# A hardware loop over graphs with two turns in its body in place of one

## The reference: what is computed

```
x = _layernorm(x + _L0_gnn_ref(x, L0_gnn_a, adj, adj), axis=-1)
x = _layernorm(x + _L1_gnn_ref(x, adj, L1_gnn_Wp, ..., L1_gnn_b2), axis=-1)
x = _layernorm(x + _L2_gnn_ref(x, adj, L2_gnn_W, L2_gnn_e, L2_gnn_bias), axis=-1)
x = _layernorm(x + _L3_gnn_ref(x, adj, L3_gnn_W, L3_gnn_a_src, L3_gnn_a_dst), axis=-1)
```

## Time and profile before

| what | value |
|---|---|
| median of 3 runs | 1199.27 us (1198.74 to 1199.39) |
| the profiled execution: its own time | 1201.41 us |
| the profiled execution: span on the core | 1199.5 us |
| share of the span busy: PE, DVE, ACT, POOL | 93%, 90%, 84%, 34% |
| granted TensorE clock over the span | 0.97 of full speed, 1.00 in the loop |

### The profile page before, as it was taken

How to read it: one execution, slowest core, us unless ns; L and a number is a source line. 1 busy time by engine, 2 the same in 40 slices (tenths; PEclk the granted TensorE clock), 3 DMA queues, 4 the chain that set the end, 5 groups by cost and what they waited for, 6 DMA issues and landing times.

```text
span 1199.5 us, 29294 instructions
## 1 busy us (share of the span) xinstructions
PE 1115.1 (93%) x7721; PEld 913.9 (76%) x7752; DVE 1082.1 (90%) x4214; ACT 1012.0 (84%) x2581; POOL 405.5 (34%) x800
## 2 busy tenths in 40 slices
PE   4778999999999999999999999999999999999864
PEld 3456788888777778888777788887777788878653
DVE  6898999999999999999999999999999999997542
ACT  3456799999999999999999999999999999998654
POOL 3122334423334344323433344233343443233211
PEclk9699999999999999999999999999999999999876
DMA  3000011011011111010011110110111100100000
GB/s 84 27 19 28 27 37 36 20 33 35 17 35 35 35 35 33 20 35 26 26 35 35 35 35 17 35 35 18 35 35 35 35 27 25 36 27 11 19 9 18
DMA packets 59459, 35.95 MB, mean 30 GB/s; under 512 B 3872, under 2 KB 54816, under 8 KB 59424
## 3 DMA queue, kind: packets, MB, share of 16 engines
q1 hardware_dynamic: 59424, 35.54, 9.7%
HBM read 18.75 MB, written 8.39 MB: 23 GB/s over the span
## 4 chain that ended last, share of the span: by engine, by line
DVE 46%; issue 28%; POOL 12%; PE 8%; ACT 2%; DVEq 2%; POOLq 0%; DMA 0%; ACTq 0%; SPq 0%
DVE wB L1116 5%; DVE pTB L1147 5%; DVE vA L1226 4%; DVE wE L1116 3%; DVE vA L1245 3%; DVE wE L1134 3%; POOL rirA L450 3%; POOL lnr_E L438 2%; POOL lnr_B L438 2%; DVE lnst_B L1268 2%; DVE lnst_D L1088 2%; DVE lnst_C L1088 2%; DVE t2B L1301 2%; DVE lnst_Z L1088 1%; DVE y_D L1318 1%
## 5 line engine op out<-in xcount | busy, mean ns | idle before, releaser
L750 PE MATMUL ps<-hE,pTE 128*128 128x128 f32 x1024 | 133.7, 279 | 0.1
L432 POOL TENSOR_TENSOR lnve_Z<-lnmv_Z,consts 128x4 f32<-128x4 f32 x32 | 17.1, 534 | 330.8 <-DVE lnmv_Z L1096 330.8
L678 PE MATMUL ps<-xsA,pA 128*128 128x128 f32 x1024 | 124.3, 281 | 1.2 <-ACT xsA L1555 1.2
L750 PE MATMUL ps<-hB,pTB 128*128 128x128 f32 x1024 | 124.9, 275 | 0.0
L750 PEld LDWEIGHTS ps<-hE,pTE 128*128 128x128 f32 x1024 | 122.8, 193 | 2.3 <-issue 0.6
L810 PE MATMUL ps<-att_j,xD 128*128 128x512 f32 x256 | 124.3, 609 | 0.0
L767 PE MATMUL ps<-gin_j,hgat 128*128 128x512 f32 x256 | 121.7, 599 | 0.0
L678 PEld LDWEIGHTS ps<-xsA,pA 128*128 128x128 f32 x1024 | 119.1, 195 | 1.5 <-ACT xsA L1555 1.3
L750 PEld LDWEIGHTS ps<-hB,pTB 128*128 128x128 f32 x1024 | 119.4, 192 | 0.2 <-issue 0.2
L1116 DVE SCALAR_TENSOR_TENSOR wE<-ps,hE,y2E 128x512 f32<-128x512 f32 x128 | 90.0, 745 | 24.8 <-ACT y2E L1577 21.5
L1545 ACT ACTIVATE pA<-vA,nmA,rirA 128x512 f32<-128x512 f32 x128 | 104.6, 818 | 4.7 <-DVE vA L1245 4.7
(11 more groups left out here) (237 smaller groups left out, 3040.9 us busy)
## 6 DMA issues: line engine op xcount, KB each, us to landing
xA<-in_x_dram SPq DMA_DIRECT2D x32, 256.0 KB, 2.6
xrA<-in_x_dram SPq DMA_DIRECT2D x32, 256.0 KB, 2.7
xrB<-xB SPq DMA_DIRECT2D x32, 256.0 KB, 2.2
out_dram<-xout SPq DMA_DIRECT2D x32, 256.0 KB, 2.2
adj_i<-in_adj_dram SPq DMA_DIRECT2D x1, 1024.0 KB, 5.2
a<-in_L_gnn_a_dram SPq DMA_DIRECT2D x2, 64.0 KB, 5.6
w_sb<-in_L_gnn_W_dram SPq DMA_DIRECT2D x2, 64.0 KB, 4.5
l2w<-in_L_gnn_W_dram SPq DMA_DIRECT2D x2, 64.0 KB, 3.7
```

Of the source, the lines that this page charges most:

```text
L678: last = mm(at("aggA")[:, i * P:(i + 1) * P], pA[:, j, i * P:(i + 1) * P], xsA[:, j], start=(j == 0), stop=(j == NT - 1))
L750: last = mm(at("agg" + n)[:, i * P:(i + 1) * P], att[n]["pT"][:, i, j], att[n]["h"][:, j, 0:P], start=(j == 0), stop=(j == NT - 1))
```

## The change

The loop goes over every second turn, and its body holds two turns, the second with the loop's register plus one. It makes 13 passes (turns 6, 8, ..., 30) in place of 26. The order of the steps on every engine and all that they compute stay the same.

```
-            with eng.Fori(LAST_DELAY + 1, GRAPHS) as it:
+            with eng.Fori(LAST_DELAY + 1, GRAPHS - 1, 2) as it:
                 body(Turn(it, GRAPHS))
+                body(Turn(it + 1, GRAPHS))
```

## The result

The changed kernel takes 1240.4 us (median of six runs, 1236.7 to 1244.2). The kernel before took 1199.3 us on the same chip (median of six, 1198.7 to 1199.9). The ratio is 1.034, with a 95% interval of 1.0328 to 1.0353: slower by 41.1 us. The profiled execution of the changed kernel took 1241.05 us, with a span of 1239.2 us.

A forecast was written before the change was run, and what follows sets the result against it. DVE was taken to set the pace: 36.0 us of refetch stalls at 12 jumps less 2.0 us for removed branches gave +34 us, 1199.3 to 1233 us; range 1195.5 to 1254 us, likeliest case alone 1218 to 1250 us.

The forecast's parts named there:

- likeliest case: DVE alone refetches code at its jump back: 1233 us (1218 to 1250), chance 0.52.
- DVE sets the pace, and its place before `lnve_B` is what the change touches.: Steady loop: PE and ACT wait for DVE every turn; DVE's 0.30 us idle at the back edge is affected.
- DVE's pass no longer fits, and the head is fetched again at 12 jumps.: DVE's pass grows from 192 to 371 instructions, 1.5 to 2.9 packets; its first piece is lost at each jump back.
- everything fits: Rival: DVE's store keeps the pass, no refetch; 1197.3 us (chance 0.25) or, with more gain, about 1195.5 us (0.10).
- Idle of 3.3 us, 3.0 more than before, 36.0 us.: Before `lnve_B` at 12 jumps back, 0.30 us idle becomes a 3.3 us fetch, priced from a 64 KB DMA: 36.0 us.
- Nothing else on it is shortened while it stands: the others catch up and wait for it: During DVE's fetch stalls, the other engines only wait, so all 36.0 us of added idle lie on the path.
- The bounds of the fetch: Added idle at DVE's 12 jumps back: 24.0 us at 2.3 us per fetch, 50.4 us at 4.5 us.
- Gain of 2.0 us from the removed edges.: DVE's 13 removed branches save 0.15 us each, limited by a chain over ACT and PE; ends 0 and 4.8 us.
- the sign that was named: Profile after: first turn of a body against second, `y_E` to `cenA`, 8.5 us without a branch, 8.7 with it.
- the second turn's saved register operations: Fewer register operations in a body's second turn, issued beside running work: counted at nothing, at most 0.7 us back.
- The branches of ACT, PE, POOL and SP cost nothing.: Back edges on the engines other than DVE cost nothing now; ACT's lies within 0.87 us of waiting for PE.
- ACT misses too: Rival: ACT also refetches at its back edge, 2.1 us per jump reaching DVE, 26 us more, 1259 us; ACT or PE 0.13.

The follow-up runs named there:

- place 13: Changed kernel with DVE's loop head moved to instruction 13 of its 128-instruction packet, so a pass ends with the third packet: 1192.56 us, 0.9945 of the kernel before.
- the delay on DVE: Changed kernel with DVE's loop head at the start of a packet and two needless multiplications on DVE ending each pass: 1229.53 us, 1.0248 of the kernel before.
- place 8: Changed kernel with DVE's loop head moved to instruction 8 of its 128-instruction packet, so a pass touches three packets: 1191.67 us, 0.9942 of the kernel before.
- the padded kernel: Changed kernel, DVE's head at 8 in its packet, ACT's pass lengthened by 60 fulfilled waits, ACT's head at 111, touching four packets: 1266.63 us.
- place 14: Changed kernel with DVE's loop head at instruction 14 of its packet, so only the branch lies in a fourth packet: 1256.65 us, 1.0472 of the kernel before.
- ACT padded, place 60: Changed kernel, DVE's head at 8 in its packet, ACT's pass lengthened by 60 fulfilled waits, ACT's head at 60, touching three packets: 1212.67 us.

## Why the prediction was right, and where its sizes were off

The forecast was 1233 us; 1240.4 us came, within the range and within the likeliest case's own (1218 to 1250 us). The mechanism was right. That the number is so close owes something to luck: the fetch was put 4.8 us too high and the clock's 14.2 us were missing, and the two errors partly cancel. Point by point:

- **DVE sets the pace, and its place before `lnve_B` is what the change touches.** Right. DVE alone doubled gives 1.0328, all others doubled 0.9993.
- **DVE's pass no longer fits, and the head is fetched again at 12 jumps.** Right, and so was the reason: four touched packets plus the one ahead are five, and the store holds four. The place at which it decides was sharper than the text said: not the 2.9 packets of code, but where in a packet the loop begins. The rival "everything fits" was given the condition that the store holds four or five packets; that contradicts this count, since with four and the head behind place 13 the kernel misses unless it is hinted, and with four and the head at place 13 or before it fits. And the 129 instructions to a packet were counted from the 20 packets within the span, while six more of 8 KB had come in the 11 us before it; the places 13 and 14 give 128.
- **Idle of 3.3 us, 3.0 more than before, 36.0 us.** The idle is 2.90 us, 2.60 more, 31.2 us. The row taken, a load of 64 KB, was 0.4 us too slow a stand-in; the small load's 2.3 us was 0.6 us too fast a one.
- **"Nothing else on it is shortened while it stands: the others catch up and wait for it".** This is the step that was incomplete. The others did wait, and PE's wait cost its clock: 14.2 us that no term of the sum had. The bounds of the fetch (24.0 to 50.4 us) took it in only by their width. The profile of before could not show it, since PE nowhere stood more than 0.4 us in the loop, but it is a second price of stalls of that length, and the delay on DVE, without any fetch, showed its lighter kind by itself (7 us where PE stood 2.05 us).
- **Gain of 2.0 us from the removed edges.** In the changed kernel the remainder is 3.9 us, about 6.5 us with the 0.2 us of each second turn counted apart. Where nothing is fetched again (place 8) the sign that was named came as forecast: 8.51 us from `y_E` to `cenA` without a branch (567.08 to 575.59), 8.67 us with it (533.17 to 541.84). But the pass of two turns is 67.52 us in place of 68.04, 0.52 us shorter and not 0.15. The missing part lies behind `cenA`: in the second turn 0.16 us ahead of `wE`, in each of the two turns 0.05 us ahead of `wB`, and less than 0.1 us in small pieces. The prediction had counted the second turn's saved register operations at nothing since they stand beside running work; ahead of `wE`, which follows short instructions, they don't.
- **The branches of ACT, PE, POOL and SP cost nothing.** Right (0.9993).
- **"Everything fits", 1197.3 us.** It didn't happen, but the kernels at places 8 and 13 are that case: 1191.7 and 1192.6 us, faster than its forecast by the undersized gain of 0.5 us per pass, about 7 us over the loop (877.4 in place of 884.4 us). So most of that case's chance belonged on the side of faster by more than 0.2%, not on no change.
- **"ACT misses too", 26 us on top.** It didn't happen in the changed kernel. Forced, it cost 54 us: the price of 2.1 us per jump relied on slack that the padded kernel no longer had, and again the clock was not in the sum.

The rule of the Trainium skill that was weighed there (Runtime: NRT & Kernel Launch, Instruction fetch mechanics) named the right engine, DVE and not PE. The other one (Advanced Engine Details and Errata, Control Flow Timing, about 108 ns for a compare-and-branch) would have made the gain 1.4 us by the estimate there; the runs have 0.23 to 0.32 us of idle at a steady jump that hits, counter and registers included, and at place 8 the loop is 7.0 us shorter.

## What to carry to other kernels

Before making a loop's body longer, count the instructions of one pass on each engine, waits and register operations too, and add the place of the loop's head within its packet (0 is its first instruction): on DVE a sum of 384 fitted here and 385 didn't (on ACT 352 fitted and 403 didn't). If it does, move the head, hint the branch, shorten the body, or write the whole loop out; here the four gave 1191.7, 1195.8, 1199.3 and 1180.1 us against 1240.4. And a stall on the engine that sets the pace has a second price: the matmul engine waits with it, and its clock can fall afterwards, which cost 1.0 or 2.6 us each time here.

## What the runs showed of the hardware

- Code comes to DVE in packets of 128 instructions, and its store holds four; ACT's rows agree with the same size (352 kept, 403 fetched again). One more than three touched on DVE, by a single instruction, took the kernel from 0.9945 to 1.0472 of the time before.
- A jump to a packet that is gone costs DVE 2.8 to 3.2 us of idle, and 3.9 to 4.2 us at place 14, where another fetch had begun 0.3 to 0.6 us before. After one miss the whole pass is fetched again, five packets.
- A hint at the branch keeps four packets in place without any fetch (1195.8 us in place of 1240.4).
- PE standing 2.05 to 2.8 us once in 70 us was enough to lose the upper clock in 7 to 10 of 12 passes, mostly at 1.0 us, up to 2.6 us each; with 3.5 to 3.8 us it was lost in all twelve (place 14), with 1.6 us (ACT padded, place 60) it was kept through the whole loop.
- 30 instructions with two fulfilled waits each, with the loop's counter and branch, held ACT for 2.5 us, at most some 80 ns each.
